# Softmax attention in a four-block kernel: both normalisations and every second copy of transposed probabilities move to ScalarE, and a bias moves from TensorE to VectorE

## What is computed

```python
def _L1_attn_ref(x, Wq, Wk, Wv):                 # x is layernorm of the stream
    q, k, v = x @ Wq.T, x @ Wk.T, x @ Wv.T
    score = softmax(q @ k.T) / sqrt(128)         # 512 x 512 for each sequence
    return score @ v

def _L1_ffn_ref(x, wr, br, w1, b1, w2, b2):      # x is layernorm of the stream
    expert_id = argmax(x @ wr + br)              # one of 8 for each token
    h = gelu(x @ w1[expert_id] + b1[expert_id])
    return h @ w2[expert_id] + b2[expert_id]
```

## Time and profile before

| | us |
|---|---|
| median of 3 runs | 1647.91 (1646.39 to 1648.25) |
| the profiled execution | 1648.63 |
| its span, first to last instruction | 1646.8 |
| PE busy | 1358.9 (83%) |
| DVE busy | 1048.7 (64%) |
| ACT busy | 745.1 (45%) |
| POOL busy | 691.5 (42%) |
| mean granted clock of PE | 0.94 |

### The profile page before, as it was taken

How to read it: one execution, slowest core, us unless ns; L and a number is a source line. 1 busy time by engine, 2 the same in 40 slices (tenths; PEclk the granted TensorE clock), 3 DMA queues, 4 the chain that set the end, 5 groups by cost and what they waited for, 6 DMA issues and landing times. The chain is left out here.

```text
span 1646.8 us, 34410 instructions
## 1 busy us (share of the span) xinstructions
PE 1358.9 (83%) x10706; PEld 1040.7 (63%) x10706; DVE 1048.7 (64%) x3598; ACT 745.1 (45%) x1519; POOL 691.5 (42%) x865
## 2 busy tenths in 40 slices
PE   3899999999849999999999556643888888299997
PEld 1566666666627888888888445532665556188886
DVE  3678777787547888888888636662788877201100
ACT  2445545455327676766767233331333333044332
POOL 2344444443300435353535438882334343234443
PEclk9999999999759999999999779986999999599999
DMA  2222122220030000000000066531400000375550
GB/s 77 34 31 39 21 37 29 28 38 16 12 103 1 17 24 19 19 23 16 26 13 26 17 214 186 174 106 51 129 27 36 29 35 31 136 253 196 182 177 11
DMA packets 65752, 108.62 MB, mean 66 GB/s; under 512 B 9767, under 2 KB 34395, under 8 KB 65296
## 3 DMA queue, kind: packets, MB, share of 16 engines
q1 hardware_dynamic: 54416, 82.27, 19.0%
q0 software_dynamic: 11264, 25.46, 4.3%
HBM read 65.34 MB, written 36.04 MB: 62 GB/s over the span
## 5 line engine op out<-in xcount | busy, mean ns | idle before, releaser
L1124 DVE TENSOR_TENSOR m_Sl<-m_S,m_Sh 128x512 fp32r<-128x512 f32 x256 | 174.3, 690 | 32.4 <-ACT m_S L1034 27.6
L1034 ACT ACTIVATE m_S<-PS,W 128x512 f32<-128x512 f32 x256 | 175.7, 686 | 25.5 <-PE PS L942 22.5
L1570 PE MATMUL PS<-f_xT,f_wt 128*128 128x256 f32 x480 | 123.3, 394 | 42.8 <-ACT f_xT L1606 42.8
L1378 POOL DMA_INDIRECT rows<-r_row,r_posi x128 | 130.5, 1019 | 35.7 <-issue 35.7
L1365 POOL TENSOR_TENSOR r_soft<-r_euler,r_soft 128x32 f32<-128x32 f32 x16 | 86.8, 5428 | 133.2 <-DVE r_soft L1270 133.2
L1029 ACT ACTIVATE m_Sh<-PS,W 128x512 fp32r<-128x512 f32 x128 | 88.2, 689 | 106.2 <-PE PS L942 105.9
L735 DVE TENSOR_TENSOR am<-PS,C 128x512 f32<-128x512 f32 x192 | 119.4, 676 | 20.9 <-PE PS L427 20.9
L1581 PE MATMUL PS<-f_wt,f_hid 128*128 128x128 f32 x960 | 130.9, 279 | 1.8 <-ACT f_hid L1619 1.8
L1655 DVE TENSOR_TENSOR f_res<-PS,f_row 128x256 f32<-128x256 f32 x40 | 17.0, 424 | 181.1 <-PE PS L1585 181.1
L1581 PEld LDWEIGHTS PS<-f_wt,f_hid 128*128 128x128 f32 x960 | 122.7, 191 | 11.1 <-ACT f_hid L1619 2.0
L1570 PEld LDWEIGHTS PS<-f_xT,f_wt 128*128 128x128 f32 x480 | 87.2, 195 | 58.5 <-ACT f_xT L1606 35.6
(11 more groups left out here) (233 smaller groups left out, 3280.9 us busy)
## 6 DMA issues: line engine op xcount, KB each, us to landing
f_row<-rows SPq DMA_DIRECT2D x80, 260.0 KB, 2.7
f_wt<-wr SPq DMA_DIRECT2D x40, 514.0 KB
f_wt<-wr SPq DMA_DIRECT2D x40, 256.0 KB, 3.1
rows<-r_padding SPq DMA_DIRECT2D x32, 260.0 KB, 3.2
X<-x SPq DMA_DIRECT2D x16, 256.0 KB, 5.6
qr<-qphi SPq DMA_DIRECT2D x64, 64.0 KB
kr<-kphi SPq DMA_DIRECT2D x64, 64.0 KB
X<-mid SPq DMA_DIRECT2D x16, 256.0 KB, 2.9
```

The costliest lines, as they stand in the source:

```text
L1034: nc.scalar.activation(S[:, n % 3, :], PS[:, n % 3, :], ACT.Silu, bias=w("b1")[:, n:n + 1]).then_inc(s_ready, 1)
L1124: nc.vector.tensor_tensor(Sl[:, n % 4, :], S[:, n % 3, :], Sh[:, n % 4, :].bitcast(F32), ALU.subtract).then_inc(sl_ready, 1)
L1378: nc.gpsimd.indirect_dma_start(out=self.rows, out_offset=bass.IndirectOffsetOnAxis(ap=self.posi[:, u, t:t + 1], axis=0), in_=self.row[:, u ...
L1570: mm = nc.tensor.matmul(PS[:, 2 + 2 * (u % 2) + bank, half * SLOT:(half + 1) * SLOT], wt[:, u, f * P:(f + 1) * P], xT[:, u % 2, :], start= ...
```

## The change

- In softmax attention the normalisation of batch b + 1 and the routing normalisation of batch b - 1 move from DVE to ACT, as x * rstd + shift with shift = -mean * rstd. POOL works out the shift with two more small multiplications, before and after the power. ACT also copies the token numbers into the rows. The routing of the first layer is untouched but for one more constant.
- The copies of transposed probabilities of tiles 1 and 3 move from DVE to ACT; PE waits for `pT_copied` for these.
- ACT's list becomes: exps(0), routing normalisation, exps(1), normalisation of b + 1, exps(2), copy_p(1), copy of routing transposes, copy of the transposes of b + 1, exps(3), copy of plain rows, copy_p(3), copy of y, copy of v.
- DVE's list becomes: largest(0), routing statistics, largest(1), statistics of b + 1, copy_p(0), largest(2), largest(3), copy_p(2), pick, place, reciprocals, residual. PE's and POOL's lists keep their order.
- In the second routed layer b2 comes with the weights, spread over all partitions (128 more columns), and DVE adds it to the plain rows before it adds PE's result; the matmuls with the row of ones and the transfers of b2 go.

```diff
@@ Routing
     def dve_statistics(self, dve, b, u, turn):
+        if self.layer:
+            after_previous(dve, self.shift_ready, b)
@@
+    def act_normalise(self, act, b, u, turn):
+        nc = self.nc
+        act.wait_ge(self.shift_ready, b + 1)
+        if not isinstance(turn, int) or turn:
+            act.wait_ge(self.scattered[u], 16 * CT * turn)
+        nc.scalar.activation(self.row[:, u, :, COL_ID:COL_ID + 1], self.c("ids")[:, bass.ds(b * CT, CT)].unsqueeze(2), ACT.Copy)
+        for t in range(CT):
+            xt = self.X[:, bass.ds(b * CT + t, 1), :].rearrange("p o d -> p (o d)")
+            ins = nc.scalar.activation(self.row[:, u, t, 0:P], xt, ACT.Identity, bias=self.shift[:, t:t + 1],
+                                       scale=self.rstd[:, t:t + 1])
+        ins.then_inc(self.xn_ready, 1)
@@ pool_inverse_deviation
         pool.wait_ge(self.ln_stats, b + 1)
+        if self.layer:
+            after_previous(pool, self.xn_ready, b)
+            nc.gpsimd.tensor_tensor(self.below[:, :], self.mv[:, :, 0], self.minus_one[:, :], ALU.mult)
         nc.gpsimd.tensor_tensor(self.ve[:, :], self.mv[:, :, 1], self.eps[:, 0:CT], ALU.add).then_inc(self.ve_done, 1)
         pool.wait_ge(self.ve_done, b + 2)
         nc.gpsimd.tensor_tensor(self.rstd[:, :], self.ve[:, :], self.minus_half[:, :], ALU.pow).then_inc(self.rstd_ready, 1)
+        if self.layer:
+            pool.wait_ge(self.rstd_ready, b + 1)
+            nc.gpsimd.tensor_tensor(self.shift[:, :], self.below[:, :], self.rstd[:, :], ALU.mult).then_inc(self.shift_ready, 1)
@@ routed
-                if layer:
-                    sp.dma_start(b2r[0:1, u, :], b2[bass.ds(e, 1), :]).then_inc(weights_in[u], 16)
@@
-                    if layer:
-                        mm = nc.tensor.matmul(PS[:, 6 + v, a * P:(a + 1) * P], one_row[:, :], b2r[0:1, u, :],
-                                              start=False, stop=True)
@@
-            def add_x(s, u):
+            def add_x(s, u, turn):
+                v = u % 2
+                dve.wait_ge(weights_in[u], 16 * (turn + 1))
+                if since(s, 2):
+                    dve.wait_ge(res_ready, s - 1)
+                nc.vector.tensor_tensor(xb[:, v, :, :], row[:, u, :, COL_X:COL_X + P],
+                                        wt[:, u, B2:B2 + P].unsqueeze(1).to_broadcast([P, 2, P]), ALU.add).then_inc(xb_ready, 1)
+                dve.wait_ge(xb_ready, s + 1)
                 dve.wait_ge(out_psum, s + 1)
-                nc.vector.tensor_tensor(res[:, u, :, :], PS[:, 6 + u % 2, 0:SLOT].rearrange("p (a d) -> p a d", a=2),
-                                        row[:, u, :, COL_X:COL_X + P], ALU.add).then_inc(res_ready, 1)
+                nc.vector.tensor_tensor(res[:, u, :, :], PS[:, 6 + v, 0:SLOT].rearrange("p (a d) -> p a d", a=2),
+                                        xb[:, v, :, :], ALU.add).then_inc(res_ready, 1)
@@ softmax_attention, tensor
+                    free = (pT_ready, pT_copied)[t % 2]
@@ softmax_attention, scalar
                 exps(0)
+                route(0)
                 exps(1)
+                turn(0)
                 exps(2)
-                route(0)
-                turn(0)
-                exps(3)
+                copy_p(1)
                 route(1)
                 turn(1)
+                exps(3)
+                route(2)
+                copy_p(3)
                 turn(2)
-            stages(act, f, a, steps(act, routing.act_copy_xT, routing.act_copy_x))
+                turn(3)
+            stages(act, f, a, steps(act, routing.act_normalise, routing.act_copy_xT, routing.act_copy_x))
@@ softmax_attention, vector
                 copy_p(0)
-                route(1)
                 largest(2)
-                turn(1)
-                copy_p(1)
                 largest(3)
                 copy_p(2)
+                route(1)
                 route(2)
-                copy_p(3)
-                route(3)
                 invert()
                 add_residual()
```

More of the change, by code:

```diff
@@ L117, in program @@
         with ExitStack() as sems:
-            routed(0, sems=sems, rows=rows_dram[0], weights=wr0, b2=None, dest=mid_dram, stored=stored[0], **slots, **shared)
+            routed(0, sems=sems, rows=rows_dram[0], weights=wr0, dest=mid_dram, stored=stored[0], **slots, **shared)
             softmax_attention(sems=sems, mid=mid_dram, rows=rows_dram[1], scattered=scattered[1], **slots, **shared)
-            routed(1, sems=sems, rows=rows_dram[1], weights=wr1, b2=br2, dest=out, stored=stored[1], **slots, **shared)
+            routed(1, sems=sems, rows=rows_dram[1], weights=wr1, dest=out, stored=stored[1], **slots, **shared)
 def clear_semaphores(nc):
@@ L1162, in __init__ @@
         self.rstd = sb("rstd", [P, CT])
+        self.shift = sb("shift", [P, CT])
+        self.below = sb("below", [P, CT])
+        self.minus_one = sb("minus_one", [P, CT])
         self.row = sb("row", [P, buffers, CT, ROW])
@@ L1195, in __init__ @@
         self.rstd_ready = sem("rstd_ready")
+        self.shift_ready = sem("shift_ready")
         self.xn_ready = sem("xn_ready")
@@ L1445, in sp_padding, with routed @@
         sp.wait_ge(self.padded, 16 * (SPARE // SLOT + EXPERTS))
-def routed(layer, nc, sems, X, w, c, PS, before, ones, minus_half, eps, scratch, rows, weights, b2, dest, slot_row, slot_expert, stored):
+def routed(layer, nc, sems, X, w, c, PS, before, ones, minus_half, eps, scratch, rows, weights, dest, slot_row, slot_expert, stored):
     chunks = (2, 4)[layer]
     B1 = 2 * chunks * P
+    B2 = B1 + chunks
     with ExitStack() as ctx:
@@ L1565, in up @@
             def up(s, u, turn):
[L1566 removed]
+                pe.wait_ge(weights_in[u], 16 * (turn + 1))
                 pe.wait_ge(xT_ready, s + 1)
@@ L1582, in down @@
                                               wt[:, u, (chunks + f) * P:(chunks + f + 1) * P],
-                                              start=(f == 0), stop=(f == chunks - 1 and not layer))
-                    if layer:
-                        mm = nc.tensor.matmul(PS[:, 6 + v, a * P:(a + 1) * P], one_row[:, :], b2r[0:1, u, :],
-                                              start=False, stop=True)
+                                              start=(f == 0), stop=(f == chunks - 1))
                 mm.then_inc(out_psum, 1)
@@ L1716, in softmax_attention @@
         rstd = sb("rstd", [P, CT])
+        shift = sb("shift", [P, CT])
+        below = sb("below", [P, CT])
+        apart = sb("apart", [P, 1])
         xn = sb("xn", [P, CT, P])
@@ L1776, in rstd_step @@
                     pool.wait_ge(ln_stats, b + 1)
+                    after_previous(pool, xn_ready, b)
+                    nc.gpsimd.tensor_tensor(below[:, :], mv[:, :, 0], routing.minus_one[:, :], ALU.mult)
                     nc.gpsimd.tensor_tensor(ve[:, :], mv[:, :, 1], eps[:, 0:CT], ALU.add).then_inc(ve_done, 1)
@@ L1779, in rstd_step @@
                     nc.gpsimd.tensor_tensor(rstd[:, :], ve[:, :], minus_half[:, :], ALU.pow).then_inc(rstd_ready, 1)
+                    pool.wait_ge(rstd_ready, b + 1)
+                    nc.gpsimd.tensor_tensor(shift[:, :], below[:, :], rstd[:, :], ALU.mult).then_inc(shift_ready, 1)
                 return [rstd_step]
@@ L1884, in copy_y, with normalise @@
                     nc.scalar.activation(yT[:, u, :], PS[:, 1, :], ACT.Copy).then_inc(y_ready, 1)
-                return [copy_x, copy_y, copy_v]
+                def normalise():
+                    act.wait_ge(shift_ready, b + 1)
+                    after_previous(act, xT_psum, b)
+                    for t in range(CT):
+                        xt = X[:, bass.ds(b * CT + t, 1), :].rearrange("p o d -> p (o d)")
+                        ins = nc.scalar.activation(xn[:, t, :], xt, ACT.Identity, bias=shift[:, t:t + 1],
+                                                   scale=rstd[:, t:t + 1])
+                    ins.then_inc(xn_ready, 1)
+                return [normalise, copy_x, copy_y, copy_v]
             def a(b, u, nxt, sent):
@@ L1921, in stats @@
                 def stats():
-                    dve.wait_ge(x_in, 16 * b + 16)
+                    after_previous(dve, shift_ready, b)
+                    wait_apart(dve, nc, x_in, 16 * b + 16, apart)
                     for t in range(CT):
@@ L1928, in stats @@
                     ins.then_inc(ln_stats, 1)
[L1930 to L1937, removed]
+                return [stats]
             def a(b, u, nxt, sent):
@@ L1991, in _ @@
             routing.dve_begin(dve)
-            stages(dve, f, a, steps(dve, routing.dve_statistics, routing.dve_normalise, routing.dve_pick, routing.dve_place))
+            stages(dve, f, a, steps(dve, routing.dve_statistics, routing.dve_pick, routing.dve_place))
             routing.dve_end(dve)
```

29 lines of the change are left out of this document (17 added, 12 removed).

## The result

The changed kernel takes 1672.16 us (median of 4 runs, 1670.90 to 1674.17) against 1647.61 us before: a ratio of 1.0151, 95% interval 1.0133 to 1.0169. It is 24.6 us slower. The profiled execution has a span of 1671.1 us and a mean granted clock of 0.919.

A forecast was written before the change was run, and what follows sets the result against it. Bound: attention's routing normalisation waits for POOL's deviation behind its scatters; in the second routed layer, TensorE never pauses. 1648.6 + 41.3 (queue) + 5.6 (ends) + 24.8 (clock) - 32.0 (routed) = 1688.3, less 0.7: 1688 us, range 1655 to 1712.

The forecast's parts named there:

- The queue on ACT: Attention: exps(1) queues behind the normalisation waiting for POOL's shift; loop 19.5 against 16.54 us, +41.3 over 14 batches.
- The steps: Attention, after the position cast: scatters end 5.29, shift ready 7.01, exps(1) starts 8.76, attend(1) 9.59 us.
- The clock: Attention: TensorE idles 4.95 us before attend(1), then runs about 4 us at half clock; +1.8 us a batch, +24.8.
- Rival 1: Attention: ACT blocks but TensorE's clock holds; 1663 us, chance 0.22.
- rival 2: Attention: the clock falls and does not return within the batch, +6.9 us a batch; 1760 us, chance 0.04.
- The ends: Attention: first normalisation +1, batch 0 +1.4, batch 1 +2.1, last batch's routing +1.1; together +5.6 us.
- What the lighter DVE brings: Attention: normalisations and copies leaving DVE are worth nothing while exps(1) is late.
- The second routed layer: Removing bias matmuls saves PE 0.82 us a slot, 39 times, -32.0 us; slot 4.08 us.
- Rival 3: Attention: ACT's order does not bind, loop 17.3 us, +0.8 a batch; faster, 1630 us, chance 0.07.
- Rival 4: Second routed layer: DMA bounds it, so the 32 us do not come in full; 1704 us, chance 0.05.

The follow-up runs named there:

- e4_filler: The changed kernel, ACT's order kept, with five unused score-sized matmuls on PE between score(2) and attend(1); 1646.32 us, ratio 0.9985.
- e3_act_order: The changed kernel with both normalisations on ACT placed after exps(2); 1636.89 us, ratio 0.9919 to the kernel before.
- e8_copies_on_act: As e7_old_order_ahead, with only the copies of transposed probabilities of tiles 1 and 3 moved to ACT; 1582.17 us, ratio 0.9595.
- e10_ahead_filler: The changed kernel with POOL's scatters one batch later and three unused matmuls on PE between score(2) and attend(1); 1614.12 us, ratio 0.9810.
- e7_old_order_ahead: The kernel before with the change's routed layer and POOL's scatters one batch later, behind the next deviations; 1582.32 us, ratio 0.9595.
- e1_routed_only: The kernel before with only the second routed layer of the change; 1600.93 us, ratio 0.9713.

## Why the prediction was right, and where it was not

**The queue on ACT** (forecast +2.95 us a batch at full clock, +41.3). Shown. The steps were 5.29, 7.01, 8.76 and 9.59 us after the position cast; the trace has 5.29, 7.04, 8.84 and 9.65. With the clock held, e4_filler has a loop of 19.35 where the sum had 19.5, so the term measures 2.76 a batch, 38.6 us. That the place in ACT's list holds attend(1) back is shown by e3_act_order, where the same instructions stand lower in the list and attend(1) is back beside the scatters. It is 1.6 of the 2.76; the other 1.1 is the longer normalisation itself, which the prediction put at 0.8 in its third rival. The sum has two small slips: its steps add up to 19.54, 3.00 above 16.54, where 2.95 is carried on, and the old loop is 16.59 in the mean.

**The clock** (forecast +1.8 us a batch, +24.8, bounds 0 and 2.8). Shown: it measures 2.0 a batch in the mean, 28 us, and 1.4 to 2.9 in single batches (loops of 20.8 to 22.2 against 19.35). In the batch shown the stretch is 4.3 us (attend(1) at 1313.08 to about 1317.4) for the 4 assumed, and from attend(1) to the count it is 10.49 us for 8.73 + 1.8. e4_filler took 26 us away by keeping PE busy. Rival 1 (the clock holds) had 0.22 and fell; so did rival 2, for it came back in every batch. The rule of the Trainium skill ("TensorE: Matmul & The Clock Gate", section "HAM oscillation — how this bites in real kernels") by which a wait between bursts makes each burst start cold is borne out here, by 26 us.

**The ends** (forecast +5.6). The stage cost 71.8, and 14 x (21.35 - 16.59) = 66.6 of it are the loop; 5.2 remain, and which end has how much was not looked for. That the three terms together meet the measured 71.8 to 0.1 us is luck: the queue was 3 us too dear and the clock 3 us too cheap.

**What the lighter DVE brings** (forecast nothing while exps(1) is late). Shown by DVE's waits of 8.0 us a batch, and for the copies by e8_copies_on_act even where exps(1) is not late.

**The second routed layer** (forecast -32.0). Here the size was off: it gave -45.8 in the trace and -47.5 alone. The failing term is "their share of PE's time is 0.41 us, twice a slot". It took the distance from the start of the bias group to the start of the next as its whole price. The full groups beside it were slower too: the eight matmuls before the slot's first bias group 0.99 instead of 0.90, those between its two 1.09 instead of 0.90, and 0.05 at the rest of the slot; 0.82 + 0.28 + 0.05 is about the 1.17 us that a slot lost. The rows for it stood in the old trace: the same eight matmuls at 1.09 us between two bias groups, while in the first routed layer, which has no bias, the next group starts 0.89 us after the same eight (1047.32 to 1048.21):

```profile
1047.32 1.05 PE L1581 MATMUL PS<-f_wt,f_hid 128*128 128x128 f32 x8
1048.21 0.38 PE L1562 MATMUL PS<-C,f_row 128*128 128x128 f32 x2
```

The other steps of this part hold: DVE's added operation is hidden, the DMA engines keep up, POOL has room.

**The whole.** 1688 was forecast and 1672 came, inside the range of 1655 to 1712. Of the 16 us, 14 are the routed term and 1.6 lie before the attention stage. Rival 3 (faster, because the order on ACT does not bind) is refuted by e3_act_order, 35 us faster by that order alone. Rival 4 (the transfers bound the routed layer) is refuted by the busy stretch at 258 GB/s. My expectation of e3_act_order failed by one step as well: it took the clock for granted at 1.00 as soon as the long gap was gone. A wait of 2.2 us at the routing transposes beside that of 1.25 at attend(0) was enough for it to fall in some of the batches.

What stays open: e10_ahead_filler is 7 us below its expected time. Its loops are 17.4 us instead of 17.7, which is about 4 of them; the rest is no more than executions and chips differ by (its profiled execution came to ACT's table load of the attention at 1125.1 us, 5.4 earlier than that of before, through code that is the same in both). Why the clock fell in some batches of e3_act_order and not in others stays open, and so does why one-row groups slow their neighbours: both were measured, not explained.

## What to carry to other kernels

A step that waits for a slow helper belongs on an in-order engine behind the work that does not need it: ask for each moved wait what is queued behind it, and look at when the awaited engine gets to it (here POOL, after 5.3 us of scatters), not at how busy the giving engine was. Price a new gap on TensorE twice, once for its length and once for the half-clock stretch after it; filling it with dead work shows the second part. A wait that carries no work of its own (here the scatter ahead of the deviations) is better taken out by order than by moving load: one batch of lag on POOL brought 19 us (e7_old_order_ahead against e1_routed_only), the two copies moved off DVE none, and the normalisations moved to ACT cost 1.1 us a batch even where nothing queued behind them.

## What the runs showed of the hardware

- The granted clock can fall with gaps much shorter than the one that made me expect it: 2.2 us and 1.25 us a batch in e3_act_order gave 0.92 over the stage, with some batches warm and others not, while before, with waits of at most 1.6 us at the routing transposes and 1.3 at attend(0), it stayed at 1.00 over 1162 to 1395 us.
- Unused matmuls in the gaps made three kernels faster by 15 to 31 us, with no other change to the work, and the clock stood at 1.00 in all three.
- A float32 group of one contraction row and 128 columns takes 0.41 us where a group of 128 rows takes 0.22, and the eight full matmuls beside it take 0.1 to 0.2 us longer. Here one row was dearer than 128, not cheaper.
